# Rotary attention with gathered expert rows: the sums of sequence n taken in beat n - 4 itself, and the fifth gather ahead of the masks of values

## The reference

```python
x = x + tanh(g_ffn[0]) * moe_top2(layernorm(x))          # 8 experts, two per row
x = x + tanh(g_xattn[1]) * rotary_attention(layernorm(x), ctx_1024)
...
q = larope((layernorm(x) @ Wq + bq).heads(16)); k = larope((ctx @ Wk + bk).heads(16))
out = softmax(q @ k.T / 8 + mask) @ v @ Wo + bo
```

## Time and profile before

| | us |
|---|---|
| three runs: median (lowest to highest) | 1485.81 (1484.23 to 1488.09) |
| the profiled execution, its own time | 1479.61 |
| its span in the trace | 1477.9 |
| PE busy | 1229.7 (83%) |
| DVE busy | 739.5 (50%) |
| ACT busy | 559.6 (38%) |
| POOL busy | 457.2 (31%) |

### The profile page before, as it was taken

How to read it: one execution, slowest core, us unless ns; L and a number is a source line. 1 busy time by engine, 2 the same in 40 slices (tenths; PEclk the granted TensorE clock), 3 DMA queues, 4 the chain that set the end, 5 groups by cost and what they waited for, 6 DMA issues and landing times. The chain is left out here.

```text
span 1477.9 us, 27400 instructions
## 1 busy us (share of the span) xinstructions
PE 1229.7 (83%) x8512; PEld 983.8 (67%) x8513; DVE 739.5 (50%) x2663; ACT 559.6 (38%) x1343; POOL 457.2 (31%) x879
## 2 busy tenths in 40 slices
PE   4699999999995999989999996465878854499991
PEld 3466667777654888888888995233656534499991
DVE  4687767777751688544122222366967722122212
ACT  2265656566661332333333331113545530133330
POOL 3334444444433344310000002557653122220004
PEclk9799999999997999999999998657989985799996
DMA  5768676666614900111111113552633204572103
GB/s 119 166 152 236 163 200 152 160 143 167 144 57 152 358 29 33 51 51 32 35 37 37 35 35 114 130 122 74 149 66 86 36 29 151 183 255 72 37 29 121
DMA packets 128725, 162.48 MB, mean 110 GB/s; under 512 B 15556, under 2 KB 113484, under 8 KB 123724
## 3 DMA queue, kind: packets, MB, share of 16 engines
q1 hardware_dynamic: 120184, 133.67, 34.0%
q0 software_dynamic: 8416, 27.27, 5.5%
HBM read 103.23 MB, written 55.19 MB: 107 GB/s over the span
## 5 line engine op out<-in xcount | busy, mean ns | idle before, releaser
L761 DVE CUSTOM_DVE_ANT_0 att_masked_scores<-att_S,Bm 128x256 bf16<-128x256 f32 x512 | 192.5, 419 | 68.3 <-PE att_S L507 54.2
L644 ACT ACTIVATE att_PT<-att_T 128x512 f32<-128x512 f32 x256 | 151.3, 595 | 93.5 <-PE att_T L526 84.5
L2383 ACT ACTIVATE moe_hT<-moe_H,moe_b 128x128 f32<-128x128 f32 x312 | 89.0, 368 | 194.6 <-PE moe_H L2298 194.0
L2298 PE MATMUL moe_H<-moe_aT,ff_w 128*128 128x128 f32 x1248 | 148.9, 279 | 6.4 <-DVE ff_w L2581 5.7
L2298 PEld LDWEIGHTS moe_H<-moe_aT,ff_w 128*128 128x128 f32 x1248 | 147.9, 195 | 9.4 <-DVE ff_w L2581 6.9
L2310 PE MATMUL moe_Z<-moe_W,moe_hT 128*128 x624 | 142.7, 382 | 0.8 <-DVE moe_z L2588 0.8
L2310 PEld LDWEIGHTS moe_Z<-moe_W,moe_hT 128*128 128x128 f32 x624 | 115.4, 190 | 15.6 <-issue 1.2
L507 PE MATMUL att_S<-L_KS,L_QS 96*128 96x256 bf16 x512 | 99.2, 276 | 21.7 <-DMA L_KS<-att_k_dram 16.6
L1348 POOL DMA_INDIRECT out_g<-yd,dest x32 | 31.2, 974 | 275.3 <-POOLq L52 266.6
L2588 DVE TENSOR_TENSOR moe_z<-moe_Z,moe_b 128x256 f32<-128x256 f32 x39 | 16.5, 424 | 196.3 <-PE moe_Z L2310 196.3
L526 PE MATMUL att_T<-L_QS,L_KS 99*128 99x256 bf16 x512 | 98.4, 273 | 0.0
(11 more groups left out here) (424 smaller groups left out, 2312.4 us busy)
## 6 DMA issues: line engine op xcount, KB each, us to landing
xd<-zero SPq DMA_DIRECT2D x14, 1280.0 KB
moe_W<-in_L_ffn_W SPq DMA_DIRECT2D x16, 1024.0 KB, 13.2
em_W<-in_L_ffn_W POOLq DMA_DIRECT2D x14, 1024.0 KB, 6.9
att_q_dram<-att_pq SPq DMA_DIRECT2D x16, 384.0 KB
att_k_dram<-att_pk SPq DMA_DIRECT2D x16, 384.0 KB, 2.6
L_QS<-att_q_dram SPq DMA_DIRECT2D x16, 384.0 KB, 4.8
L_KS<-att_k_dram SPq DMA_DIRECT2D x16, 384.0 KB, 8.0
moe_xs<-xd SPq DMA_DIRECT2D x39, 128.0 KB, 2.0
```

Source lines behind the costliest of these rows:

```text
L644: nc.scalar.activation(PT[:, h % 8, :], bankT[h % 2][:, :], ACT.Exp).then_inc(exp_done, 1)
L761: ins = nc.vector.tensor_tensor_reduce(masked_scores[:, h % 2, u, :], bankS[h % 2][:, u * SEQ:(u + 1) * SEQ], masks[m // B][0][:, u * SEQ: ...
L2298: ins = nc.tensor.matmul(bankH[half][:, f * P:(f + 1) * P], w1s[:, cc, g * P:(g + 1) * P], xT[:, s % 2, cc * P:(cc + 1) * P], start=(cc == ...
L2383: ins = nc.scalar.activation(eT[:, s % 2, g * P:(g + 1) * P], bankH[half][:, f * P:(f + 1) * P], ACT.Relu, bias=b1[:, bass.ds(e * NF + g, 1)])
```

## The change

Two things move, and one order with them.

- On DVE, the two sums and the moments of sequence b + 5 stood at h = 5, 6 and 14 of beat b. Those of sequence b + 4 now stand at h = 0, 1 and 2 of beat b; the norm of its rows moves from h = 2 to h = 9. In the fill, the sums and moments of sequence 4 at h = 13 and 14 of beat -1 are gone.
- On POOL, `gather(4)` is issued in front of the masks of sequences 0 to 2.
- On POOL, in each beat the parts of the queries now stand in front of the input roots.

PE's, ACT's and SP's programs are the same.

```diff
--- before.py
+++ after.py
@@ -1374,16 +1374,16 @@
             parts(2, 0)
             input_roots(3)
             parts(2, 1)
+            gather(4)
             pool.wait_ge(kept_in, 1)
             for m in range(3):
                 keep_values(m)
-            gather(4)
             gather(5)
             for b in range(0, M + 2):
+                if has(b + 3):
+                    parts(b + 3, 0)
                 if has(b + 4):
                     input_roots(b + 4)
-                if has(b + 3):
-                    parts(b + 3, 0)
                 if has(b - 2):
                     inverse_roots(nc, pool, t, moments, root_step, b - 2).then_inc(rooted, 1)
                 if has(b + 3):
@@ -1546,10 +1546,6 @@
                     value_rows(2)
                 if h == 11:
                     input_norm(3)
-                if h == 13:
-                    sum_rows(4)
-                if h == 14:
-                    input_moments(4)
             for b in range(0, M + 2):
                 for h in range(H):
                     if has(scores_of(b, h)[0]):
@@ -1559,26 +1555,26 @@
                         queries(b + 3)
                     if h == 1 and has(b - 2):
                         row_stats(b - 2)
+                    if h == 0 and has(b + 4):
+                        sum_experts(b + 4, 0)
+                    if h == 1 and has(b + 4):
+                        sum_experts(b + 4, 1)
                     if h == 2 and has(b + 4):
-                        input_norm(b + 4)
+                        input_moments(b + 4)
                     if h == 4 and has(b + 3):
                         turned_keys(b + 3)
-                    if h == 5 and has(b + 5):
-                        sum_experts(b + 5, 0)
-                    if h == 6 and has(b + 5):
-                        sum_experts(b + 5, 1)
                     if h == 7 and has(b + 1):
                         minus_maxima(b + 1)
                     if h == 8 and has(b + 3):
                         value_rows(b + 3)
                     if h == 9 and has(b + 1):
                         max_columns(b + 1)
+                    if h == 9 and has(b + 4):
+                        input_norm(b + 4)
                     if h == 9 and has(b - 2):
                         norm(b - 2)
                     if h == 12 and has(b - 1):
                         output_rows(b - 1)
-                    if h == 14 and has(b + 5):
-                        input_moments(b + 5)
                     if h in TURN_AT and 0 <= turning < QUADS * M:
                         normalise(turning)
```

## The result

The changed kernel is slower: 1492.91 us median of five runs (1489.51 to 1496.78), against 1484.23 us for five runs of the kernel before (1477.63 to 1488.09). The ratio is 1.0067, with a 95% interval of 1.0039 to 1.0095. The prediction was 1492.3 us, slower with a chance of 0.65; the point and the direction hold.

What follows compares the result with a forecast made beforehand. POOL's chain up to the key sum was taken to bound the fill and beats 2 and 3. Terms -1.2 + 3.4 + 3.8 + 0.5 = +6.5 us gave 1486.1, moved by 6.2 to the median's level: 1492.3; range 1484.0 to 1498.5.

Steps and rivals of the forecast that it cites:

- What bounds the fill: Up to beat 0's key sum: POOL's gapless work sets the time, so removing DVE's 16.22 us stall gains 1.0 us.
- so the rows are there at 1002.3: Gather 4 in the fill: rows usable 6.64 us after the first issue at 995.7, DVE waiting some 3 us.
- Beats 0 and 1: Gain of 1.2 us together, between 3 us of gain and 1 us of loss.
- the key sum comes 5.1 + 3.8 = 8.9 us behind it: Beat 1: query parts and roots separate query step and key sum, 6.8 us before, so 2.0 us are given back.
- Beats 2 and 3: Input roots lengthen query step to key sum to 13.4 us; losses 3.4 and 3.8 us.
- what I said would show it: Among the signs of a right forecast: ACT's waits for the key sum grow to some 8 us in beats 2 and 3.
- Clock, and beat 4: PE's lower clock after longer stalls costs 0.5 us, between 0 and 1.6; beat 4, without input roots, changes nothing.
- The faster one: POOL's backlog doesn't hold beat 0; its key sum starts some 12 us earlier, total 1480.3 us; chance 0.11.
- that of no difference: Roots find cover in beats 2 and 3 because something else holds PE; 1484 us; chance 0.16.
- The worse one: POOL's adds block DVE's sums, 2.9 us a pair; 2.8 us more in each of beats 2 and 3; 1498; chance 0.1.

Runs made afterwards that it cites:

- the experiment on the input roots: The changed kernel without POOL's input roots of sequences 5, 6 and 7; ratio 0.9998 to the kernel before.

## Why the prediction was right

**What bounds the fill: right.** POOL's row of work gave 1.0 us, not 16: the key sum of beat 0 was forecast 28.6 us behind the maxima of h = 13 and came after 28.6. Leaving the masks out of the changed kernel showed the row to be the bound. The gather's landing was wrong in the step "so the rows are there at 1002.3": 10.0 us from the first issue, not 6.64, so DVE waited 6.93 us and not 3. It cost nothing because DVE was not the bound.

**Beats 0 and 1: the sign was wrong, by 2.2 us.** Up to the query step of beat 1 I had 2.0 us of gain; it was 2.5. The step that failed is "the key sum comes 5.1 + 3.8 = 8.9 us behind it": it took 10.3. I had taken a pair of sums for 1.50 us; beside POOL's adds it took 1.88 and 1.77, and DVE's key step and ACT's second part came late enough to hold POOL. Instead of -1.2 us the two beats gave 33.73 + 25.41 - 34.76 - 23.35 = +1.0. None of my cases had DVE's key step holding POOL.

**Beats 2 and 3: right.** 13.4 us from query step to key sum was forecast for each, 13.5 measured, and its parts as well: the input roots of beat 2 start 5.8 us behind the query step, and two chains of 3.9 and 3.8 us follow. By the table it is +2.9 and +3.8 us for 3.4 and 3.8; the window of beat 2 is 32.90 us for about 33.5. Without the input roots the loss went away. Wrong was what I said would show it, that ACT's waits would grow to 8 us: the sums at h = 0 and 1 held PE and ACT back by about as much as the roots held POOL, so the wait stayed near 4 us; without the sums it was 7.50. A wait that doesn't grow does not acquit the engine waited for.

**Clock, and beat 4:** 0.5 us were set for the clock, and "beat 4 takes the same". By the table beat 4 took 0.9 more. It starts at the key sum of beat 3, so the value projection of that beat lies in it, 3.58 us for 3.20. And the programs are not the same in it: in the changed kernel the norm of sequence 7 stands at h = 9 of beat 3, and PE waits for it before it turns those rows, which it did not in the kernel before:

```profile
1125.45 0.66 PE L1057 MATMUL out_A<-ident,Y 128*128 128x128 f32 x4 [0.42 <-DVE Y L151]
```

I had priced the norm's new place in beat 0 alone. Sum: +1.0 + 2.9 + 3.8 + 0.9 = +8.65, for a forecast of +6.5; nearly the whole miss is that of beats 0 and 1. That 1492.3 came so near 1492.91 owes something to the median of before, which moved from 1485.81 to 1484.23 with two more runs: that is luck, worth 1.6 us.

**The rivals.** The faster one fell with the key sum of beat 0, that of no difference with the experiment on the input roots. The worse one was priced by each of four sums waiting out an add, 2.9 us a pair. Measured beside the adds: 1.88 and 1.77 us in beat 1, 1.88 and 0.85 in beat 2. The rule of the Trainium skill ("SBUF — State Buffer", "SBUF: two separate sides"), by which such a DVE operation and a GpSimd one that reads SBUF block each other, agrees in direction: each pair was slowed when it ran with an add. In beat 2 the second pair ran in a gap but for its first 0.2 us and took 0.85 us.

## What to carry to other kernels

Before a wait is taken away, look which queue reaches the next meeting point last: a stall of 16 us on DVE was worth 1 us, because POOL's row of work beside it had no gap. When small work moves to a later step "half a beat later", write down what now stands between the last input and the first output that another engine takes in its own order; here 3.8 us of roots went into that stretch, and the better edit was to move something out of it (the output roots, 11.5 us). And a change made for the fill can be applied to the fill alone; here that alone was worth some 3 us, at the edge of what the times can tell.

## What the runs showed of the hardware that I had not expected

Four indirect gathers issued some 6 us earlier brought their rows only 2 to 3 us earlier: first issue to first use went from 6.6 us to between 9.9 and 11.1, with SP's stacking transfers issued between them. Issued 13 us earlier, beside another stacking, they took 9.7 us. That the stacking is the cause was not tried. And the pair of 128 x 256 sums on DVE, 0.87 us alone, took up to 1.88 us with POOL's 128 x 512 adds running, more than the 1.50 us of the trace before.
